# Splitting the value products of seven head groups by head and placing each head behind a quarter of a neighbouring projection

## The chip, the cores and the metric

One core of one Trainium2 chip. The metric is the time on the device of one execution, in microseconds (us). The kernel is written by hand: each engine has its own instruction stream, in an order fixed in the source, and the engines meet only through semaphores.

## What is computed

16 batches of x (256 tokens, 512 channels) go through three blocks, each followed by a residual sum and a layer norm (the inputs are float32):

```python
def _L0_attn_ref(h, Wq, bq, Wk, bk, Wv, bv, Wo, bo):        # 16 heads of 32 channels
    q, k, v = h @ Wq.T + bq, h @ Wk.T + bk, h @ Wv.T + bv   # (reshaped to heads)
    scores = jnp.einsum('bqhd,bkhd->bhqk', q, k) * scale    # causal
    attn = jax.nn.softmax(scores, axis=-1)
    o = jnp.einsum('bhqk,bkhd->bqhd', attn, v).reshape(B, S, H)
    return o @ Wo.T + bo

def _L0_ffn_ref(x, W_gate, W_qkv):                          # one shared key and value head
    indicator = one_hot(argmax(softmax(x @ W_gate.T)))
    q, k, v = jnp.split(x @ W_qkv.T, 3, axis=-1)
    k_shared = jnp.einsum('bth,bthd->btd', indicator, k)
    v_shared = jnp.einsum('bth,bthd->btd', indicator * top1_val, v)
    return causal_attention(q, k_shared, v_shared)

x = _layernorm(x + _L0_attn_ref(x, ...))
x = _layernorm(x + _L0_xattn_ref(...))     # a linear recurrence over time (wkv)
x = _layernorm(x + _L0_ffn_ref(x, ...))
```

## The kernel before

The program is a pipeline over batches. `iteration(t)` works on two of them at once: the first attention ("a", batch t) and the gated attention ("f", batch t-1), with the first projections of batch t+1 at its end. Iterations 1 to 14 have all three parts; the first and the last two lack some.

**What TensorE does.** In each iteration there are these kinds of work:

- Projections. One job is 12 matmuls of 512 columns (`tokens_out`) or 24 of 256 columns (`channels_out`), since each product is made of three: high by high, high by low and low by high part (`products`, L389 to L396). All of them write one PSUM bank, `pp`. The next job may start only when ScalarE and VectorE have taken the last one out of it: that is counted by `pa_free` (attention) and `pf_free` (gated). For a query or key job ScalarE writes the high part and then VectorE the low part (`qk_lo`, L1144). For the keys and values of the gated part VectorE multiplies by the gate (`pick`, L1202). For the output projection (`PA_WO`) VectorE adds the bank to the residual (`first_residual`, L1171). The second layer norm's result is transposed partly into `pp` too, and VectorE's second L1133 frees it. `PA_WO` waits besides for `a_free`: its moving side `k_lo` comes from L1157.
- Scores. There are four head groups of four heads in each attention. For each group the scores are made twice: in `sq` (L426 to L437) for the row maxima, which VectorE takes (L1015, then L1019 and L1020 for `neg_parts`); the maxima are transposed (`max_transpose`, L445), copied and carried into the operand by a DMA; and in `sk` (L461 to L472), of which ScalarE makes the exponentials (L819) into `prob0` and `prob1`.
- Values. One group is `values` (L476 to L490): for each of its four heads three float32 products of 33 columns (L484, L486, L488; each is two instructions in the trace), 24 instructions. They write `po`. VectorE then normalises (L1050, L1051), which counts `a_norm` or `f_norm`; in the gated part L1221 adds it to the residual (`third_residual`).
- Transposes of x, of y, of the outputs (L497) and of the shared key (L584, once for each iteration: its start serves below as the border of an iteration).

**What sets the order.** The order on each engine is that of the calls in `iteration`. SyncE's queue has the DMAs that stack q and k (L258) for the next batch, in a fixed order too. The value groups stand where they are called: a0 to a3 for the attention, f0 to f3 for the gated part. In an iteration from border to border the order of those with their neighbours is: a3 then `PF_V+1`; f0 then `PA_WO`; f1 then `PA_Q+1`; f2 then `PA_K+1`; f3, then the first scores of the next batch and `PA_V`; a0; a1 then `PF_Q`; a2 then `PF_K+1`.

Of the kernel before, what the change touches and what calls it, by code (L numbers as in the profile page):

```python
# [7 lines left out]
P = 128  # L8
CC = D // P
TT = S // P  # L10
NG = 4
# [28 lines left out]
def build(nc, x_d, xT_d, ctxT_d, weights_d, gate_d, ch_bias_d, row_bias_d, decay_d, first_d, out_d):  # L40
# [18 lines left out]
    with ctx:  # L59
# [328 lines left out]
        def _(pe):  # L388
            def products(out, lhs, rhs):  # L389

                for c in range(CC):
                    (lh, ll), (rh, rl) = lhs(c), rhs(c)
                    T.matmul(out, lh, rh, start=(c == 0), stop=False, skip_group_check=True)  # L393
                    T.matmul(out, lh, rl, start=False, stop=False, skip_group_check=True)  # L394
                    mm = T.matmul(out, ll, rh, start=False, stop=(c == CC - 1), skip_group_check=True)  # L395
                return mm  # L396
# [7 lines left out]
            def channels_out(w, pair):  # L404

                for i in range(2):
                    mm = products(pp[:, S * i:S * (i + 1)], weight(w, P * (2 * pair + i), P), tokens(0, S))
                return mm

            def tokens_out(bank, w, c, hi_t=xt_hi, lo_t=xt_lo):  # L410

                return products(bank[:, 0:D], tokens(P * c, P, hi_t, lo_t), weight(w, 0, D))
# [63 lines left out]
            def values(b, g, value, s_exp, s_norm, s_po):  # L476

                if g:
                    pe.wait_ge(s_norm, NG * b + g)
                pe.wait_ge(s_exp, TILES * b + 3 * (g + 1))  # L480
                out = po[:, 0:TT * HG * (HD + 1)].rearrange("p (c h d) -> p c h d", c=TT, h=HG)
                for k in range(HG):
                    h = HG * g + k
                    T.matmul(out[:, 0, k, :], prob0[:, k, 0:P], value(0, h),  # L484
                             start=True, stop=True, skip_group_check=True)
                    T.matmul(out[:, 1, k, :], prob0[:, k, P:S], value(0, h),  # L486
                             start=True, stop=False, skip_group_check=True)
                    mm = T.matmul(out[:, 1, k, :], prob1[:, k, :], value(1, h),  # L488
                                  start=False, stop=True, skip_group_check=True)
                mm.then_inc(s_po, 1)  # L490
# [51 lines left out]
            def project_a(b, job):  # L542

                weight_split(b, (W_Q, W_K, W_V, W_O)[job // 2])
                if job == PA_Q:
                    pe.wait_ge(xt_ready, b + 1)
                if job == PA_WO:

                    wait(pe, pf_free, PF_JOBS * b)

                    pe.wait_ge(a_free, A_JOBS * (b + 1))
                if job != PA_WO:
                    wait(pe, pa_free, PA_JOBS * b + job)
                if job < PA_K:
                    mm = channels_out(W_Q, job - PA_Q)
                elif job < PA_V:
                    mm = channels_out(W_K, job - PA_K)
                elif job < PA_WO:
                    mm = tokens_out(pp, W_V, job - PA_V)
                else:  # L560
                    mm = tokens_out(pp, W_O, job - PA_WO, k_hi, k_lo)
                mm.then_inc(pa_job, 1)

            def project_f(b, job):
# [6 lines left out]
                if job < PF_K:  # L571
                    mm = channels_out(W_FQ, job - PF_Q)
                elif job < PF_V:
                    mm = tokens_out(pp, W_FK, job - PF_K)
                else:
                    mm = tokens_out(pp, W_FV, job - PF_V)
                mm.then_inc(pf_job, 1)

# [41 lines left out]

            def values_a(b, g):
                values(b, g, value_a, a_exp, a_norm, a_po)

            def values_f(b, g):
                values(b, g, value_f, f_exp, f_norm, f_po)

            def iteration(t, do_a, prev, nxt):
# [65 lines left out]
                if do_a:  # L693
                    values_a(t, 3)
                if prev:
                    max_f(b, 0)
                    project_f(b, PF_V + 1)
# [10 lines left out]
                if prev:  # L708
# [6 lines left out]
                    values_f(b, 0)  # L715
                    if do_a:
                        max_f(b, 1, a_free, A_JOBS * a_done)
                if do_a:
                    project_a(t, PA_WO)
# [14 lines left out]
                if prev:  # L734
                    if not nxt:
                        max_f(b, 2)
                    values_f(b, 1)
                    if nxt:
                        max_f(b, 2)
                if nxt:  # L740
                    project_a(t + 1, PA_Q + 1)
# [11 lines left out]
                if prev:  # L753
                    if not nxt:
                        max_f(b, 3)
                    values_f(b, 2)
                    if nxt:
                        max_f(b, 3)
                if nxt:
                    project_a(t + 1, PA_K + 1)  # L760
                if prev:
# [3 lines left out]
                    values_f(b, 3)  # L765
# [6 lines left out]
                if nxt:  # L772
# [6 lines left out]
                    project_a(t + 1, PA_V)  # L779
# [789 lines left out]
```

## Time and profile before

| | |
|---|---|
| median of 3 runs | 1965.76 us (1945.75 to 1984.34) |
| profiled execution, span from first to last instruction | 1963.6 us; its own time is not listed apart; the span is 2.2 us under the median |
| TensorE | busy 1781.0 us, 91% |
| VectorE | busy 1268.9 us, 65% |
| ScalarE, GpSimdE | 24%, 27% |
| granted TensorE clock, mean | 0.837 |

PE is TensorE, PEld its weight loads, DVE VectorE, ACT ScalarE, POOL GpSimdE, SP SyncE. PEclk is the TensorE clock that was granted, as a share of full speed; it has two levels, 0.5 and 1.0 (1.2 and 2.4 GHz), so that a mean says how long each held. In a timeline row stand the start, the time taken, the engine, the line, the operation, what it writes and reads, and in brackets how long the engine stood idle before it and who released it.

### The profile page before, as it was taken

What the parts mean: (1) busy time and instruction counts of PE and PEld (TensorE: products, weight loads), DVE (VectorE), ACT (ScalarE), POOL (GpSimd) and SP (SyncE); (2) the same over time, 40 slices, a digit from 0 to 9 for tenths busy, and PEclk for the clock granted to TensorE, in tenths of its full rate; (3) what the DMA queues carried; (4) which work ended last, traced back from release to release, by engine and by line L of the source; (5) the groups of instructions that cost most, each with busy time, mean ns of one, the idle gap of its engine ahead of it and who ended that gap; (6) DMA issues with size and microseconds to landing.
All of it is one profiled execution on the core that took longest, in us unless ns stands there. A gap on an engine that the chain in (4) does not pass through costs nothing.

```text
span 1963.6 us, 33890 instructions
## 1 busy us (share of the span) xinstructions
PE 1781.0 (91%) x11904; PEld 1596.7 (81%) x11904; DVE 1268.9 (65%) x2678; ACT 477.5 (24%) x1040; POOL 521.0 (27%) x701
## 2 busy tenths in 40 slices
PE   5769989999999999999899999989899999999767
PEld 4658878888888888888888888878788888888656
DVE  3356766858576685757668575776848575685743
ACT  2232222313222132322222132221323132132201
POOL 1033230504133050323315041230505033050400
PEclk8679989788887878898797887988898886878675
DMA  5223122322213132221213222131322212131010
GB/s 139 82 62 82 42 77 50 81 59 62 73 25 79 42 81 59 62 62 33 75 49 81 59 62 54 41 82 42 81 59 62 73 38 60 49 81 50 6 43 12
DMA packets 61494, 118.30 MB, mean 60 GB/s; under 512 B 12688, under 2 KB 31120, under 8 KB 61456
## 3 DMA queue, kind: packets, MB, share of 16 engines
q1 hardware_dynamic: 61456, 117.79, 23.5%
q8 instruction: 24, 0.39, 0.1%
q14 instruction: 14, 0.11, 0.0%
HBM read 32.81 MB, written 8.39 MB: 21 GB/s over the span
## 4 chain that ended last, share of the span: by engine, by line
PE 71%; DVE 16%; issue 5%; DMA 3%; POOL 2%; ACT 2%; SPq 1%; DVEq 0%; POOLq 0%; ACTq 0%
PE pp L393 11%; PE pp L394 10%; PE pp L395 10%; PE po L488 6%; PE po L486 6%; PE po L484 6%; PE sq L434 4%; DVE neg_max L1015 4%; PE sq L426 3%; PE sk L461 3%; PE sk L469 2%; DVE neg_parts L1019 2%; PE sq L437 2%; DMA q_stack<-max_rows 1%; PE sq L429 1%
## 5 line engine op out<-in xcount | busy, mean ns | idle before, releaser
L819 ACT ACTIVATE prob<-sk 128x512 f32<-128x512 f32 x384 | 217.3, 597 | 799.9 <-PE sk L464 599.6
L1015 DVE TENSOR_REDUCE neg_max<-sq 128x2 f32<-128x512 f32 (+1 forms) x384 | 252.5, 679 | 82.3 <-PE sq L429 55.4
L393 PE MATMUL pp<-xt_hi,w_hi 128*128 128x256 f32 x768 | 235.0, 306 | 27.9 <-DVE w_lo L1002 14.4
L394 PE MATMUL pp<-xt_lo,w_hi 128*128 128x256 f32 x768 | 225.8, 294 | 0.0
L395 PE MATMUL pp<-xt_hi,w_lo 128*128 128x256 f32 x768 | 225.4, 294 | 0.0
L393 PE MATMUL pp<-w_hi,xt_hi 128*128 128x512 f32 x384 | 184.3, 480 | 7.7 <-DVE w_lo L1002 4.2
L393 PEld LDWEIGHTS pp<-xt_hi,w_hi 128*128 128x128 f32 x768 | 156.2, 203 | 33.1 <-issue 22.3
L394 PE MATMUL pp<-w_lo,xt_hi 128*128 128x512 f32 x384 | 173.2, 451 | 0.0
L395 PE MATMUL pp<-w_hi,xt_lo 128*128 128x512 f32 x384 | 170.6, 444 | 0.0
L1432 POOL TENSOR_TENSOR xt_lo<-x_raw,xt_hi 128x1024 fp32r<-128x1024 f32 x16 | 37.7, 2354 | 454.0 <-ACT xt_hi L857 454.0
L394 PEld LDWEIGHTS pp<-xt_lo,w_hi 128*128 128x128 f32 x768 | 156.3, 204 | 0.0
L395 PEld LDWEIGHTS pp<-xt_hi,w_lo 128*128 128x128 f32 x768 | 155.8, 203 | 0.0
L1111 DVE RECIPROCAL w_key<-w_key 128x256 f32<-128x256 f32 x64 | 111.2, 1737 | 18.2 <-POOL w_key L1459 18.2
L484 PE MATMUL po<-v_f,prob 128*128 128x33 f32 x512 | 109.0, 298 | 11.7 <-ACT prob L819 11.3
L1420 POOL TENSOR_TENSOR var_eps<-meanvar,eps 128x2 f32<-128x2 f32 x48 | 9.4, 197 | 411.7 <-DVE meanvar L1062 411.7
L488 PE MATMUL po<-v_a,prob 128*128 128x33 f32 x512 | 115.1, 311 | 0.0
L488 PE MATMUL po<-v_f,prob 128*128 128x33 f32 x512 | 114.2, 309 | 0.0
L484 PE MATMUL po<-v_a,prob 128*128 128x33 f32 x512 | 108.3, 297 | 6.1 <-ACT v_a L872 3.6
L486 PE MATMUL po<-v_a,prob 128*128 128x33 f32 x512 | 113.9, 308 | 0.0
L486 PE MATMUL po<-v_f,prob 128*128 128x33 f32 x512 | 112.7, 305 | 0.0
L393 PEld LDWEIGHTS pp<-w_hi,xt_hi 128*128 128x128 f32 x384 | 87.4, 228 | 28.2 <-DVE w_val L1202 4.6
L1427 POOL TENSOR_TENSOR xa<-xa,bo_row 128x512 f32<-128x512 f32 x32 | 40.3, 1282 | 259.1 <-DMA xa<-in_x 259.1
(162 smaller groups left out, 4247.2 us busy)
## 6 DMA issues: line engine op xcount, KB each, us to landing
q_stack<-q_hi SPq DMA_DIRECT2D x256, 128.0 KB, 2.3
q_stack<-q_lo SPq DMA_DIRECT2D x128, 128.0 KB, 2.3
k_stack<-k_hi SPq DMA_DIRECT2D x128, 128.0 KB, 2.3
x_raw<-in_xT SPq DMA_DIRECT2D x16, 512.0 KB, 3.5
k_stack<-k_lo SPq DMA_DIRECT2D x64, 128.0 KB, 2.3
xa<-in_x SPq DMA_DIRECT2D x16, 512.0 KB, 3.5
w_val<-in_ctxT SPq DMA_DIRECT2D x64, 128.0 KB, 2.1
out_y<-xb SPq DMA_DIRECT2D x16, 512.0 KB, 2.9
```

Of the source, the lines that this page charges most:

```text
L393: T.matmul(out, lh, rh, start=(c == 0), stop=False, skip_group_check=True)
L394: T.matmul(out, lh, rl, start=False, stop=False, skip_group_check=True)
L395: mm = T.matmul(out, ll, rh, start=False, stop=(c == CC - 1), skip_group_check=True)
L426: T.matmul(out[:, P * k:P * (k + 1)], q_stack[0:3 * HD, h, 0:P], key(h, 0, P, 3 * HD), start=(k == 0), stop=False, skip_group_check=True)
L434: T.matmul(out[:, S * k:S * (k + 1)], q_stack[0:3 * HD, h, P:S], key(h, 0, S, 3 * HD), start=(k == 0), stop=False, skip_group_check=True)
L461: T.matmul(out[:, S * k:S * (k + 1)], key(h, 0, P, rows), q_stack[0:rows, h, :], start=(k == 0), stop=False, skip_group_check=True)
L484: T.matmul(out[:, 0, k, :], prob0[:, k, 0:P], value(0, h), start=True, stop=True, skip_group_check=True)
L486: T.matmul(out[:, 1, k, :], prob0[:, k, P:S], value(0, h), start=True, stop=False, skip_group_check=True)
L488: mm = T.matmul(out[:, 1, k, :], prob1[:, k, :], value(1, h), start=False, stop=True, skip_group_check=True)
L819: A.activation(dst, sk[n % 2][:], ACT.Exp, scale=SCALE).then_inc(s_exp, 1)
L1015: V.tensor_reduce(dst, src, AX.X, ALU.max, negate=True).then_inc(s_max, 1)
L1111: V.reciprocal(w_key[:, c % HC, :], w_key[:, c % HC, :]).then_inc(w_rec, 1)
```

## The change

`values` is cut into `values_head(b, g, k)`: the three products of one head. `products` gets a `then`, which is called after each of the first three of its four contraction steps; `channels_out` calls it in the middle and at the end of its first half and in the middle of its second. `project_a` and `project_f` call the fourth head after the job's last matmul, and after its semaphore. So a head stands behind each quarter of the projection. The call that transposes the maxima (`max_f`) stands behind the first head (at a3) or the second (at f0, f1, f2). Group a0 stays as it was. f3 moves from ahead of the first scores of the next batch to `PA_V`, behind them.

```diff
-            def products(out, lhs, rhs):
+            def products(out, lhs, rhs, then=None):
...
                     mm = T.matmul(out, ll, rh, start=False, stop=(c == CC - 1), skip_group_check=True)
+                    if then is not None and c < CC - 1:
+                        then(c)
...
+            def channels_out(w, pair, then=None):
+
+                first = None if then is None else lambda c: then(0) if c == 1 else None
+                second = None if then is None else lambda c: then(2) if c == 1 else None
+                products(pp[:, 0:S], weight(w, P * (2 * pair), P), tokens(0, S), first)
+                if then is not None:
+                    then(1)
+                return products(pp[:, S:2 * S], weight(w, P * (2 * pair + 1), P), tokens(0, S), second)
...
+            def values_head(b, g, k, value, s_exp, s_norm, s_po):
+
+                if k == 0:
+                    if g:
+                        pe.wait_ge(s_norm, NG * b + g)
+                    pe.wait_ge(s_exp, TILES * b + 3 * (g + 1))
...
+                if k == HG - 1:
+                    mm.then_inc(s_po, 1)
...
                 mm.then_inc(pa_job, 1)
-
-            def project_f(b, job):
+                if then is not None:
+                    then(HG - 1)
...
                 if do_a:
-                    values_a(t, 1)
+                    if not prev:
+                        values_a(t, 1)
                     max_a(t, 2)
                 if prev:
-                    project_f(b, PF_Q)
+                    project_f(b, PF_Q, head_a(t, 1) if do_a else None)
...
-                    values_a(t, 2)
-                if prev:
-                    project_f(b, PF_K + 1)
+                    if not prev:
+                        values_a(t, 2)
+                if prev:
+                    project_f(b, PF_K + 1, head_a(t, 2) if do_a else None)
...
-                    project_a(t + 1, PA_V)
+                    project_a(t + 1, PA_V, head_f(b, 3) if prev else None)
```

TensorE's order in the loop body, at a2 and `PF_K+1`. Names: `pt` and `po` are PSUM banks, `v_a` the values. Before, the whole group stands between the transpose of the maxima and the projection that waits for `pf_free`:

```order
L445 MATMUL pt<-ident,neg_parts 16x128 [waits a_free,a_neg]
L484 MATMUL po<-v_a,prob 128x33 [waits a_exp,a_norm]
L486 MATMUL po<-v_a,prob 128x33
L488 MATMUL po<-v_a,prob 128x33
L484 MATMUL po<-v_a,prob 128x33
...
L488 MATMUL po<-v_a,prob 128x33
L393 MATMUL pp<-w_hi,xt_hi 128x512 [waits pf_free]
L394 MATMUL pp<-w_lo,xt_hi 128x512
```

After, the projection and its wait come right behind the transpose, and a head behind every three of its matmuls:

```order
L450 MATMUL pt<-ident,neg_parts 16x128 [waits a_free,a_neg]
L393 MATMUL pp<-w_hi,xt_hi 128x512 [waits pf_free]
L394 MATMUL pp<-w_lo,xt_hi 128x512
L395 MATMUL pp<-w_hi,xt_lo 128x512
L489 MATMUL po<-v_a,prob 128x33 [waits a_exp,a_norm]
L491 MATMUL po<-v_a,prob 128x33
L493 MATMUL po<-v_a,prob 128x33
L393 MATMUL pp<-w_hi,xt_hi 128x512
L394 MATMUL pp<-w_lo,xt_hi 128x512
```

The wait for `pf_free` has moved ahead of all twelve value products.

The same engine at f0 and `PA_WO`. Before, the group comes first and the projection waits behind it:

```order
L437 MATMUL sq<-mask_qk,ident_b 128x128 x2
L220 REGISTER_ALU
L712 REGISTER_ALU [waits a_norm]
L484 MATMUL po<-v_f,prob 128x33 [waits f_exp,dve_f]
L486 MATMUL po<-v_f,prob 128x33
...
L445 MATMUL pt<-ident,neg_parts 16x128 [waits a_free]
L220 REGISTER_ALU
L393 MATMUL pp<-w_hi,k_hi 128x512 [waits a_free,pf_free]
```

After:

```order
L746 REGISTER_ALU [waits a_norm]
L220 REGISTER_ALU [waits dve_f]
L557 REGISTER_ALU [waits pf_free]
L393 MATMUL pp<-w_hi,k_hi 128x512 [waits a_free]
L394 MATMUL pp<-w_lo,k_hi 128x512
L395 MATMUL pp<-w_hi,k_lo 128x512
L489 MATMUL po<-v_f,prob 128x33 [waits f_exp]
```

The waits for `pf_free` and for `a_free` (that is `k_lo`) now stand right behind the score products, ahead of every value product.

## Rows read from the trace of the kernel before

**Rows 1.** The page, busy time of each engine over the span.
```profile
PE 1781.0 (91%) x11904; PEld 1596.7 (81%) x11904; DVE 1268.9 (65%) x2678; ACT 477.5 (24%) x1040; POOL 521.0 (27%) x701
```

**Rows 2.** Two iterations and fourteen, windows: stretch, its length, busy us, PEclk.
```profile
1226.95:1336.86 109.91, 102.80 (x745) 91.15 (x744) 78.14 (x165) 28.56 (x63) 32.49 (x43) 0.92 0.25 63
1561.50:1681.00 119.50, 114.15 (x746) 103.13 (x745) 78.37 (x165) 28.77 (x63) 32.49 (x43) 0.81 0.23 58
198.40:1795.30 1596.90, 1516.03 (x10417) 1362.69 (x10416) 1089.33 (x2310) 401.25 (x882) 454.86 (x602) 0.86 0.24 61
```

**Rows 3.** Timeline at a3 and the projection behind it.
```profile
997.97 0.36 PE L484 MATMUL po<-v_a,prob 128*128 128x33 f32 x2
999.18 0.68 DVE L1202 TENSOR_TENSOR w_val<-pp,g_ind 128x512 f32<-128x512 f32 x1
1000.65 0.47 PE L393 MATMUL pp<-w_hi,xt_hi 128*128 128x512 f32 x1
1000.96 0.39 PE L394 MATMUL pp<-w_lo,xt_hi 128*128 128x512 f32 x1
```

**Rows 4.** Timeline at a2.
```profile
1098.11 0.31 PE L484 MATMUL po<-v_a,prob 128*128 128x33 f32 x2
1100.11 0.67 DVE L1202 TENSOR_TENSOR w_val<-pp,g_ind 128x512 f32<-128x512 f32 x1
```

**Rows 5.** Timeline at a1.
```profile
1309.60 0.31 PE L484 MATMUL po<-v_a,prob 128*128 128x33 f32 x2
1310.60 0.68 DVE L1133 TENSOR_TENSOR xt_lo<-pp,xt_hi 128x512 fp32r<-128x512 f32 x1
```

**Rows 6.** Timeline at f1 and at f2.
```profile
1022.33 0.31 PE L484 MATMUL po<-v_f,prob 128*128 128x33 f32 x2
1023.13 0.87 DVE L1144 SCALAR_TENSOR_TENSOR q_lo<-pp,ch_bias,q_hi 128x256 fp32r<-128x256 f32 x2
...
1034.67 0.31 PE L484 MATMUL po<-v_f,prob 128*128 128x33 f32 x2
1034.94 0.88 DVE L1144 SCALAR_TENSOR_TENSOR k_lo<-pp,ch_bias,k_hi 128x256 fp32r<-128x256 f32 x2 [0.33 <-ACT k_hi L866]
```

**Rows 7.** Timeline at f0.
```profile
1239.54 0.27 PE L484 MATMUL po<-v_f,prob 128*128 128x33 f32 x1
1240.43 2.36 DVE L1020 TENSOR_TENSOR neg_parts<-neg_max,neg_parts 128x8 fp32r<-128x8 f32 x1
1242.71 0.47 DVE L1157 SCALAR_TENSOR_TENSOR k_lo<-pt,ch_bias,k_hi 128x256 fp32r<-128x256 f32 x1
1243.24 0.28 PE L445 MATMUL pt<-ident,neg_parts 128*16 128x128 f32 x1 [0.86 <-DVE k_lo L1157]
```

**Rows 8.** Timeline at f3; the last row is the page's on DMA issues, us to landing last.
```profile
1043.71 0.41 PE L484 MATMUL po<-v_f,prob 128*128 128x33 f32 x2 [0.69 <-ACT prob L819]
1044.49 0.59 SPq L258 DMA_DIRECT2D k_stack<-k_hi  x1
1047.22 0.45 PE L426 MATMUL sq<-k_stack,q_stack 96*128 96x128 f32 x1
...
k_stack<-k_hi SPq DMA_DIRECT2D x128, 128.0 KB, 2.3
```

**Rows 9.** VectorE behind a gated value group: first and last of three.
```profile
1028.05 0.20 DVE L1050 RECIPROCAL o_rec<-po 128x8 f32<-128x8 f32 x1
1028.74 0.42 DVE L1221 TENSOR_TENSOR xb<-xb,o_tok 128x256 f32<-128x256 f32 x1
```

**Rows 10.** Windows: four neighbouring stretches of one iteration, cut where PEclk changed.
```profile
1045.53:1055.78 10.25, 9.83 (x40) 8.18 (x40) 9.17 (x19) 2.26 (x6) 5.01 (x7) 0.50 0.67 162
1055.80:1066.00 10.20, 8.20 (x58) 6.67 (x57) 8.47 (x17) 2.77 (x5) 8.56 (x14) 1.00 0.15 33
1066.01:1086.49 20.48, 20.48 (x105) 20.10 (x105) 9.07 (x22) 3.46 (x6) 0.90 (x2) 0.50 0.19 56
1086.50:1113.80 27.30, 26.90 (x205) 24.01 (x205) 15.68 (x38) 5.88 (x14) 2.51 (x2) 1.00 0.29 70
```

More of the change, by code:

```diff
@@ L402, in tokens, with tokens_out @@
                 return lambda c: (hi_t[:, c, lo:lo + n], lo_t[:, c, lo:lo + n])
[L404 to L412, printed above, removed]
+            def channels_out(w, pair, then=None):
[5 more added lines that the diff above has]
+                return products(pp[:, S:2 * S], weight(w, P * (2 * pair + 1), P), tokens(0, S), second)
+            def tokens_out(bank, w, c, hi_t=xt_hi, lo_t=xt_lo, then=None):
+                return products(bank[:, 0:D], tokens(P * c, P, hi_t, lo_t), weight(w, 0, D), then)
             def scores_sq(b, g, tiles, stk, per, key, s_sq, s_max):
@@ L554, in project_a, with project_f @@
                 if job < PA_K:
-                    mm = channels_out(W_Q, job - PA_Q)
+                    mm = channels_out(W_Q, job - PA_Q, then)
                 elif job < PA_V:
-                    mm = channels_out(W_K, job - PA_K)
+                    mm = channels_out(W_K, job - PA_K, then)
                 elif job < PA_WO:
-                    mm = tokens_out(pp, W_V, job - PA_V)
+                    mm = tokens_out(pp, W_V, job - PA_V, then=then)
                 else:
-                    mm = tokens_out(pp, W_O, job - PA_WO, k_hi, k_lo)
+                    mm = tokens_out(pp, W_O, job - PA_WO, k_hi, k_lo, then)
                 mm.then_inc(pa_job, 1)
-            def project_f(b, job):
+                if then is not None:
+                    then(HG - 1)
+            def project_f(b, job, then=None):
                 if job == PF_Q:
@@ L571, in project_f @@
                 if job < PF_K:
-                    mm = channels_out(W_FQ, job - PF_Q)
+                    mm = channels_out(W_FQ, job - PF_Q, then)
                 elif job < PF_V:
-                    mm = tokens_out(pp, W_FK, job - PF_K)
+                    mm = tokens_out(pp, W_FK, job - PF_K, then=then)
                 else:
-                    mm = tokens_out(pp, W_FV, job - PF_V)
+                    mm = tokens_out(pp, W_FV, job - PF_V, then=then)
                 mm.then_inc(pf_job, 1)
+                if then is not None:
+                    then(HG - 1)
             def key_transpose(b, s_before, before):
@@ L692, in iteration, with piece @@
                     sq_f(b, 0, 0, 1, 2)
-                if do_a:
+                if do_a and not prev:
                     values_a(t, 3)
                 if prev:
-                    max_f(b, 0)
-                    project_f(b, PF_V + 1)
+                    if do_a:
+                        turn_third = head_a(t, 3)
+                        def piece(k):
+                            turn_third(k)
+                            if k == 0:
+                                max_f(b, 0)
+                        project_f(b, PF_V + 1, piece)
+                    else:
+                        max_f(b, 0)
+                        project_f(b, PF_V + 1)
                     wait(pe, a_exp, TILES * a_done)
@@ L733, in iteration @@
                     x1_transpose(t, 0)
[L734 to L736 removed]
+                if prev and not nxt:
+                    max_f(b, 2)
                     values_f(b, 1)
[L738 to L739 removed]
                 if nxt:
[L741 removed]
+                    project_a(t + 1, PA_Q + 1, head_f(b, 1, lambda: max_f(b, 2)) if prev else None)
                 if prev:
```

54 lines of the change are left out of this document (27 added, 27 removed).

## The prediction

> **What bounds the kernel now.** I read the busy times of the engines first. TensorE is busy 91% of the span, VectorE 65% [rows 1]: the end is set by TensorE's own stream, and a wait put into it costs its full length unless it was idle there already. Then I read the windows of single iterations. One took 109.9 us with a granted clock of 0.92, another 119.5 us with 0.81; both have the same work [rows 2]. So there are two things to spend: time in which TensorE stands still, and time at its lower clock. With levels 1.0 and 0.5, a mean of 0.92 is 17.6 us at the lower level and 0.81 is 45.4 us. 9.6 us for 27.8 us makes 0.345 us lost for each us at the lower level, and 109.9 - 0.345 x 17.6 = 103.8 us for an iteration without any. The mean iteration is 1596.9 / 14 = 114.1 us, at 0.86, some 32 us of them at the lower level [rows 2]. All that a perfect clock could give back is therefore 10.3 us an iteration.
>
> Third, the timeline around the value groups. The reader is to see what lies under them. All projections share one PSUM bank. At a3 the group starts at 997.97, and VectorE's multiply that empties the bank ends at 999.86; the projection starts at 1000.65, without a wait [rows 3]. The group, 2.65 us long, is the cover under which the bank is emptied. It is so at every moved group but f3.
>
> **The change, part by part.** The number of instructions is the same. Each projection moves ahead of its value group, and its wait for the bank with it. Behind the waiting matmul everything on TensorE queues, the value products too, which could have run. The new wait is the time from the start of the group to the end of the emptying.
> - a3: 999.86 - 997.97 = 1.9 us [rows 3].
> - a2: the gate must be worked out before VectorE can multiply; 1100.78 - 1098.11 = 2.7 us [rows 4]. Here the group was just long enough.
> - a1: both halves of the transposed x must be split first; 1311.28 - 1309.60 = 1.7 us, less about 0.1 for a transpose of maxima that runs there: 1.6 us [rows 5].
> - f1 and f2: 1024.00 - 1022.33 = 1.7 us and 1035.82 - 1034.67 = 1.15 us, of which 0.15 was a wait before as well, so 1.0 us [rows 6].
> - f0: `PA_WO` needs `k_lo`, which ended 3.6 us after the group's start, because VectorE's L1020 took 2.36 us there. The group hid 2.7 of it, 0.86 was waited for [rows 7]. Now all of it is, and the group is still to run. Cost 2.3 us, taken a little under 2.7 for the iterations in which `k_lo` comes earlier.
> - f3: the first scores of the next batch need the stacked keys. The last of the three DMAs is issued at 1044.49 and takes 2.3 us to land: 1046.8. TensorE got there at 1047.22 [rows 8]. Without f3 it gets there by 1043.7 and waits. Only 0.4 us are won, and the group's 2.65 us (full clock) come back within `PA_V`: cost 2.2 us.
>
> The group's result comes later relative to its projection: the last head now stands behind the projection's end. VectorE's stream is in order, so what is queued behind the normalising comes later too. At f0 the residual that empties the bank after `PA_WO` stands behind three operations that take 1028.05 to 1029.16, 1.1 us [rows 9]; with 0.7 us of its own and the hand-overs, `PA_WO+1` is late by about 0.95. At a2 the next multiply stands behind two of them: `PF_V` late by 0.5. At a3 the same delays the maxima of f1: 0.75. At f3 the residual, the third norm's statistics and a division stand ahead of the next maxima: 1.5. Sum of the four 3.7 us, each bounded by zero where VectorE has slack and by these values where TensorE runs at full clock.
>
> At the lower clock TensorE gets later to each such place while VectorE and ScalarE take as long as before, so waits shrink. I count a3, a2, a1 and f3 whole (1.9 + 2.7 + 1.6 + 2.2 = 8.4) and f0, f1, f2 and the four late ones by half ((2.3 + 1.7 + 1.0 + 3.7) / 2 = 4.35): 12.7 us an iteration. The ends are 8.4 and 17.1. Nothing else is added: the transposes of the maxima move by at most one group, and all of these waits come ahead of them.
>
> Seams between values and projections rise from 7 to 28 an iteration. The first matmul behind a group holds its place for 0.31 us [rows 3], where the ones in a job run at 0.23 (2.8 us for 12), so leaving a group costs 0.08; a head entered from a projection can have its first weights ready and win as much. I take zero. The Trainium skill ("TensorE: Matmul & The Clock Gate", Step-by-step: what each phase is for) says that the next weights are loaded while the running matmul streams, which would favour mixing short products with long ones; by it 21 more entries at 0.08 would win 1.7 us an iteration, 25 us in all. The row shows the price at the exit, which cancels this.
>
> **The clock.** In the rows the clock fell in stretches where value products stood next to idle time: at 1045.5, within f3 after its 0.69 us wait, and at 1066.0, within a0, and it rose again inside a projection, at 1055.8 and 1086.5 [rows 8, 10]. The stretch 1055.8 to 1066.0 that ended with the fall had only 8.20 busy us in 10.20 [rows 10]. The change works both ways. It takes away pure value stretches, which is good at full clock. But each new wait of 1.6 us or more puts idle time next to them; and once the clock is low, the next projection is half value products, and so is no longer what has brought it back. It then has to wait for the next projection that is left whole. At the lower level 105 matmul records took 20.5 us, at the upper 205 took 27.3 [rows 10], 1.5 times as long on average, and at most twice. A mixed job of 5.5 us (2.8 and 2.65) then takes 8 to 11, I take 10, the score products up to the next whole projection 5 to 7, the part of that until it rises 4. If each place falls: a2 15 us (a whole projection is near); a3 30, since `PA_WO` is mixed as well; f1 17; f3 25; a0 32, through the transposes and `PF_Q`. That is 119 us. Not every place falls each time, so I take three quarters, 90 us. No row shows a mixed projection; the ends are zero and 119.
>
> **Sum.** 103.8 + 12.7 + 0.345 x 90 = 147.6 us an iteration against 114.1: 33.5 more. Fourteen iterations have all seven groups moved and the next one four, 14.6 in all: 489 us. 1963.6 + 489 = 2453 us of span; with the 2.2 us to the median 2455 us, 25% slower.
>
> **The rivals.**
> - *The waits come, the share of the lower clock stays as it is.* What the mixing saves then equals what the waits cost. Waits halfway between 12.7 and 17.1, 14.9 us: 1966 + 14.9 x 14.6 = 2183 us. For it: the value stretches themselves are where the clock fell in before.
> - *The waits come and the clock stays up.* 103.8 + 14.9 = 118.7 us, 4.6 more: 2033 us. The whole lower-clock time goes and doesn't pay for the waits. The skill's same page (HAM oscillation) says that long pauses between bursts throttle the engine, and by it waits as short as these would not; but here the clock fell without any long pause [rows 10], so I give it little.
> - *Faster.* The mixed stretches hold the full clock and the bank is emptied sooner than the rows say, because VectorE, with the same work in a less crowded order, is no longer behind when a projection ends: waits of 5 us in place of 12.7. 103.8 + 5 = 108.8 us: 1966 - 5.3 x 14.6 = 1889 us. It decides from the point where the waits are under 10.3 us and the clock never falls. Against it: at a3, a1, f1 and f2 the emptying is a chain of its own length behind a TensorE result, not a backlog.
> - *Cancelling.* Both near 10 us, within 2% of 1966.
> - *Worse still.* All 119 us at the lower clock and each costing 0.45: 103.8 + 12.7 + 53.6 = 170 us, 2783 us.
>
> **How the numbers follow.** Forecast (2300 to 2640) 0.66; share of the clock unchanged 0.17; clock up 0.07; faster 0.04; within 2% 0.03; above 2640 0.03. The range 2130 to 2640 leaves out the last four, 0.17. A measurement of this kernel tells about 2% from no change. Faster by over 2%: 0.04; within 2%: 0.03; slower by over 2%: 0.93.
>
> **What would show it.** Right: the first matmul of `PF_K+1`, `PF_V+1`, `PF_Q`, `PA_Q+1`, `PA_K+1` and `PA_WO` with idle time ahead of it, released by VectorE's L1202, L1133, L1144 and L1157, 1 to 3.6 us each; the first scores of the next batch waiting for a DMA into `k_stack`; the mean clock falling to about 0.7, and long stretches at 0.5 that begin at such a wait and end in a whole projection. Wrong: a clock of 0.86 or above with the waits there (then 2183 or 2033), or projections that start without a wait.

## The result, and the profile after

The changed kernel takes 2504.69 us (median of 4 runs, 2494.62 to 2509.33), the kernel before 1971.39 us beside it (4 runs, 1945.75 to 1984.34). The ratio is 1.290, with a 95% interval of 1.283 to 1.298: slower. (A ratio is taken without the executions that lie over 1.5% above the fastest of their kernel, so it need not equal the quotient of the two medians, 1.270 here.) The forecast was 2455 us, 25% slower.

The page of the kernel after: span, busy times, granted clock in 40 slices.

```profile
span 2492.8 us, 33877 instructions
...
PE 2126.3 (85%) x11904; PEld 1892.3 (76%) x11904; DVE 1271.6 (51%) x2678; ACT 488.5 (20%) x1040; POOL 511.7 (21%) x701
...
PEclk8587777676676667766667776766767667786665
```

Against [rows 1] TensorE has the same 11904 instructions, and yet 2126.3 us of busy time in place of 1781.0. That is not more work but the same work at a lower clock: the mean is 0.709 where it was 0.837. The rest is standing still: 2492.8 - 2126.3 = 366 us, where it was 1963.6 - 1781.0 = 183 us. VectorE has the same busy time as before, so nothing has become dearer there.

The same fourteen iterations as in the last row of [rows 2], in a window:

```profile
214.20:2316.94 2102.74, 1845.02 (x10418) 1644.50 (x10417) 1091.84 (x2310) 411.55 (x882) 445.28 (x602) 0.71 0.18 46
```

2102.74 / 14 = 150.2 us an iteration, against 114.06. Here 36.1 x 14 = 506 us of the 529 us that the span grew.

What TensorE waited for, over the whole span (us in total, times, longest), first after and then before:

```profile
PE pp L393 <- DVE w_val L1229: 68.5, 33, 2.6
PE sq L431 <- DMA k_stack<-k_hi: 65.3, 15, 5.5
PE pp L393 <- DVE k_lo L1184: 54.6, 16, 4.3
PE pp L393 <- DVE q_lo L1171: 28.3, 18, 2.0
PE pt L450 <- DVE neg_parts L1047: 19.3, 29, 2.1
PE pp L393 <- DVE xt_lo L1160: 17.8, 16, 1.5
...
PE pp L393 <- DVE k_lo L1171: 17.8, 16, 1.9
PE sq L439 <- DVE neg_max L1042: 13.1, 28, 1.2
```

```profile
PE sq L434 <- DVE neg_max L1015: 28.5, 51, 2.4
PE pt L445 <- DVE neg_parts L1020: 28.3, 35, 2.1
...
PE pt L445 <- DVE k_lo L1157: 9.1, 11, 1.0
...
PE sq L426 <- DMA k_stack<-k_hi: 7.2, 4, 5.5
```

The new rows are those with `pp` and L393, the first matmul of a projection, and the DMA into `k_stack`. They are the seven moved groups: `w_val` is a3 and a2, `k_lo` L1184 is f0 (before it was waited for by the transpose L445), `q_lo` f1, `xt_lo` a1, `k_lo` L1171 f2, `k_stack` f3. The rows on maxima fell, 28.5 + 28.3 to 13.1 + 19.3 us.

The waits of one iteration, in the timeline of TensorE (a3, f0, the second half of `PA_WO`, f1, f2, f3, a1, a2):

```profile
1274.77 0.80 PE L393 MATMUL pp<-w_hi,xt_hi 128*128 128x512 f32 x1 [1.79 <-DVE w_val L1229]
...
1294.93 0.80 PE L393 MATMUL pp<-w_hi,k_hi 128*128 128x512 f32 x1 [3.58 <-DVE k_lo L1184]
...
1305.70 0.50 PE L393 MATMUL pp<-w_hi,k_hi 128*128 128x512 f32 x1 [1.07 <-DVE xa L1198]
...
1315.76 0.39 PE L393 MATMUL pp<-xt_hi,w_hi 128*128 128x256 f32 x1 [1.56 <-DVE q_lo L1171]
...
1328.96 0.39 PE L393 MATMUL pp<-xt_hi,w_hi 128*128 128x256 f32 x1 [1.03 <-DVE k_lo L1171]
...
1341.05 1.11 PE L431 MATMUL sq<-k_stack,q_stack 96*128 96x128 f32 x4 [4.28 <-DMA k_stack<-k_hi]
...
1381.47 0.38 PE L393 MATMUL pp<-xt_hi,w_hi 128*128 128x256 f32 x1 [1.07 <-DVE xt_lo L1160]
...
1400.51 0.65 PE L393 MATMUL pp<-w_hi,xt_hi 128*128 128x512 f32 x1 [2.56 <-DVE w_val L1229]
```

Each is at the place that the forecast named. And the clock around the first of them, in windows:

```profile
1269.61:1274.30 4.69, 2.96 (x27) 2.36 (x25) 2.92 (x7) 0.60 (x1) 0.00 (x0) 1.00 0.37 84
1274.77:1302.00 27.23, 23.65 (x98) 20.99 (x98) 9.14 (x15) 3.10 (x5) 2.34 (x1) 0.51 0.10 29
1302.20:1339.00 36.80, 30.64 (x257) 28.55 (x256) 27.01 (x57) 11.52 (x27) 12.28 (x18) 1.00 0.11 24
```

The stretch ahead is at full clock. From the wait at a3 on it is at half, through the whole mixed `PF_V+1`, the score products, the wait at f0 and three quarters of the mixed `PA_WO`: 27 us, in which 98 records ran; the next 36.8 us took 257.

### The profile page after: what moved, and what is told of

Its sections match the earlier page's. It is cut to its first block, busy times and chain, and to the rows that moved or that the text cites. A ratio compares the mean times of both kernels' runs of the same rounds, so it can differ in the third digit from the quotient of the medians.

```text
span 2492.8 us, 33877 instructions
## 1 busy us (share of the span) xinstructions
PE 2126.3 (85%) x11904; PEld 1892.3 (76%) x11904; DVE 1271.6 (51%) x2678; ACT 488.5 (20%) x1040; POOL 511.7 (21%) x701
## 4 chain that ended last, share of the span: by engine, by line
PE 78%; DVE 14%; issue 3%; DMA 2%; ACT 2%; SPq 1%; POOL 1%; DVEq 0%; POOLq 0%; ACTq 0%
PE pp L393 14%; PE pp L394 11%; PE pp L395 11%; PE po L493 7%; PE po L491 7%; PE po L489 5%; PE sq L439 4%; PE sk L466 4%; PE sq L431 3%; DVE neg_max L1042 3%; PE sk L474 3%; PE sq L434 2%; PE sq L442 2%; DMA k_stack<-k_hi 2%; DVE neg_parts L1046 2%
## 5 line engine op out<-in xcount | busy, mean ns | idle before, releaser
L1077 DVE RECIPROCAL o_rec<-po 128x8 f32<-128x8 f32 x128 | 26.4, 206 | 583.3 <-PE po L493 583.3
L393 PE MATMUL pp<-xt_hi,w_hi 128*128 128x256 f32 x768 | 248.0, 323 | 79.7 <-DVE q_lo L1171 28.3
L393 PE MATMUL pp<-w_hi,xt_hi 128*128 128x512 f32 x384 | 238.2, 620 | 72.8 <-DVE w_val L1229 68.5
L393 PEld LDWEIGHTS pp<-xt_hi,w_hi 128*128 128x128 f32 x768 | 156.8, 204 | 93.2 <-DVE q_lo L1171 28.1
L394 PE MATMUL pp<-w_lo,xt_hi 128*128 128x512 f32 x384 | 206.4, 537 | 0.0
L395 PE MATMUL pp<-w_hi,xt_lo 128*128 128x512 f32 x384 | 205.9, 536 | 0.0
L393 PEld LDWEIGHTS pp<-w_hi,xt_hi 128*128 128x128 f32 x384 | 107.4, 280 | 92.7 <-DVE w_val L1229 71.8
L489 PEld LDWEIGHTS po<-v_a,prob 128*128 128x128 f32 x512 | 128.1, 274 | 40.9 <-issue 17.2
L489 PEld LDWEIGHTS po<-v_f,prob 128*128 128x128 f32 x512 | 123.6, 263 | 23.8 <-issue 2.0
L393 PE MATMUL pp<-w_hi,k_hi 128*128 128x512 f32 x128 | 84.7, 662 | 63.6 <-DVE k_lo L1184 54.6
L493 PE MATMUL po<-v_a,prob 128*128 128x33 f32 x512 | 136.2, 356 | 0.0
L491 PE MATMUL po<-v_a,prob 128*128 128x33 f32 x512 | 134.8, 353 | 0.0
L493 PE MATMUL po<-v_f,prob 128*128 128x33 f32 x512 | 129.9, 342 | 0.0
L491 PE MATMUL po<-v_f,prob 128*128 128x33 f32 x512 | 129.8, 342 | 0.0
```

What stands on the lines that cost most here:

```text
L489: T.matmul(out[:, 0, k, :], prob0[:, k, 0:P], value(0, h), start=True, stop=True, skip_group_check=True)
L491: T.matmul(out[:, 1, k, :], prob0[:, k, P:S], value(0, h), start=True, stop=False, skip_group_check=True)
```

## The experiments

Two numbers are taken from each trace besides the time. *Idle*: the waits in brackets of TensorE's rows, summed between the starts of the first and the fifteenth shared-key transpose and divided by fourteen. *Lower level*: 2 x (1 - mean clock) x length of an iteration, the mean from the clock record of the same stretch. A *fall* is one unbroken stretch at the lower level. Before has 5.5 us idle and 31.2 us at the lower level; after has 18.3 and 86.8. Both are read from the one profiled execution of each kernel; where its clock lies at one end of that kernel's executions, the others' clocks are given.

All variants come from the changed kernel, by a helper that puts the first `mode` heads of a group ahead of its projection and the others behind its quarters. 4 is the order before, 0 that of the change; "late" puts all four behind the undivided projection. Every variant computes all of the reference.

```diff
+            def placed(mode, head, project, turn=None, at=-1):
+                if mode == "late":
+                    if turn is not None:
+                        turn()
+                    project(lambda k: [head(h) for h in range(HG)] if k == HG - 1 else None)
+                    return
+                for k in range(mode):
+                    head(k)
+                if turn is not None and at < mode:
+                    turn()
...
+                project(piece if mode < HG else None)
```

**late: the waits without the mixing.**

```diff
+MODE = {'a1': 'late', 'a2': 'late', 'a3': 'late', 'f0': 'late', 'f1': 'late', 'f2': 'late', 'f3': 'late'}
```

> Every moved group stands whole behind its undivided projection: the new waits stay, the mixing goes. If the mixed projections are what keeps the clock low once it has fallen, a fall now ends inside the next projection: mean granted clock 0.79 or more, idle time of TensorE as in the changed kernel (350 to 380 us), time 2200 to 2320 us. If the waits alone set the clock and the mixing has no part in it, the clock stays near 0.71 and the time within 2% of 2504 us.

Measured 2341.16 us (2 runs), ratio 1.201 (1.178 to 1.224), clock 0.787. A few thousandths under the clock expected and 21 us above the top of the times. Its idle time is even more than after's, 21.4 us an iteration, since the transposes of the maxima lost their cover as well. At the lower level it has 56.1 us in place of 86.8. The number of falls tells how: 9.3 an iteration of 6 us each, where after has 4.7 of 18 us and before 3.7 of 8 us. One of them, around the same place as above (`PF_V+1` behind a3's scores), in late:

```profile
1190.90 0.28 PE L452 MATMUL pt<-ident,neg_parts 128*16 128x128 f32 x1 [1.19 <-DVE neg_parts L1084]
1191.50 0.58 PE L395 MATMUL pp<-w_hi,xt_hi 128*128 128x512 f32 x1 [0.32 <-DVE w_val L1266]
1191.89 0.63 PE L396 MATMUL pp<-w_lo,xt_hi 128*128 128x512 f32 x1
...
1194.87 0.54 PE L397 MATMUL pp<-w_hi,xt_lo 128*128 128x512 f32 x1
1195.26 0.39 PE L395 MATMUL pp<-w_hi,xt_hi 128*128 128x512 f32 x1
```

The step is 0.43 us from 1191.89 on and 0.23 from 1195.26 on: here the clock is low for 3.4 us and rises within the undivided projection. In after, at the mixed one, it stayed low for 27. So with more waits than before there are more falls, with mixing or without, and with the mixing each fall is long. The time at the lower level is smaller in late although it waits more, so the mixing has a part of its own in the clock.

**half: two heads ahead as cover, two mixed, f3 put back.**

```diff
+MODE = {'a1': 2, 'a2': 2, 'a3': 2, 'f0': 2, 'f1': 2, 'f2': 2, 'f3': 4}
```

> Six groups with two heads ahead of the projection and two behind its first two quarters; f3 back ahead of the scores. Two heads cover 1.33 us of each wait. If uncovered emptying of the bank is the cause, the waits fall to 0.5 at a3, 1.3 at a2, 0.3 at a1 and f1, none at f2 and some 2 at f0, 4 to 6 us an iteration with what comes late on VectorE; clock 0.76 to 0.84; 2020 to 2150 us. If mixing as such is what costs, half of the mixing in six of seven groups keeps about 3/7 of the 530 us: 2200 us or more.

Measured 2113.48 us (2 runs), ratio 1.084 (1.045 to 1.123), clock 0.797; idle 9.9 us, lower level 46.8 us. As expected: with 1.3 us of cover left, the waits shrink and do not vanish (the wait for `w_val` is 27.4 us in all in place of 68.5).

**One place alone.** a2, f2 and f3 each changed by itself, the other six as before.

```diff
+MODE = {'a1': 4, 'a2': 0, 'a3': 4, 'f0': 4, 'f1': 4, 'f2': 4, 'f3': 4}
```

> The change at a2 alone, where the wait is longest. Waits and clock: 2.6 us of wait an iteration and a fall at each, some 12 us more at the lower level (0.345 each): 6.7 us times 15 iterations, 2060 us (2030 to 2095). An equal share of the loss for each group (mixing as such): 76 us more, 2045 us; told apart by the next run.

> The change at f2 alone, where the wait is shortest (1.0 us, and no fall of the clock in the changed kernel). Waits and clock: 1.0 us an iteration less what the clock gains from one value stretch fewer: 1945 to 1990 us. An equal share of the loss for each group: 2045 us.

> The change at f3 alone. No drain of the bank is uncovered here, but the group no longer covers the DMAs of the stacked keys: 4 us of wait for k_stack appear ahead of the next batch's first scores and 3.4 us of values with their wait leave, the group comes back within PA_V; with PA_V half value products the fall of the clock that is there anyway lasts some 10 us longer. 2.2 + 0.42 x 10 = 6.4 us an iteration, 2060 us (2020 to 2100). If only the bank's emptying counts: no change, 1930 to 1990 us.

only_a2: 2061.9 us (2 runs), ratio 1.058 (1.037 to 1.078). Its wait at the place is 2.56 us; idle 8.0, lower level 39.0 us. only_f2: 1964.47 us (10 runs), ratio 1.010 (1.002 to 1.018). Its wait is there, 1.03 us, but the lower level is 26.3 us in place of 31.2, which pays for it. (The profiled execution has a clock of 0.857; over all ten executions the mean is 0.847, over the thirteen of before beside them 0.829. The medians of all executions, 1964.47 and 1979.38 us, stand the other way round than the ratio, so whether only_f2 is a per cent slower isn't settled.) only_f3: 2069.74 us (2 runs), ratio 1.054 (1.044 to 1.065), idle 8.3 and lower level 45.6 us. All three lie within the times expected. Their rows of the new waits, in that order:

```profile
916.57 0.59 PE L395 MATMUL pp<-w_hi,xt_hi 128*128 128x512 f32 x1 [2.56 <-DVE w_val L1266]
```

```profile
910.62 0.39 PE L395 MATMUL pp<-xt_hi,w_hi 128*128 128x256 f32 x1 [1.03 <-DVE k_lo L1208]
```

```profile
PE sq L433 <- DMA k_stack<-k_hi: 59.2, 15, 5.5
```

If the split itself cost the time, each place would have a seventh of the loss, some 75 us. That falls with f2, which has all of the split and only the smallest wait: its time is within about a per cent of before's. a2 and f3, which uncover 2.6 and 3.8 us, cost five to six per cent each.

**f0_back: f0 as before, the other six as changed.**

```diff
+MODE = {'a1': 0, 'a2': 0, 'a3': 0, 'f0': 4, 'f1': 0, 'f2': 0, 'f3': 0}
```

> The whole change, but f0 back ahead of PA_WO as before. Its wait for k_lo is hidden again but for 0.65 us: 2.8 us an iteration less idle. And the first whole projection behind the fall at a3 is now PA_WO itself, so that this stretch at the lower clock ends a mixed job earlier, 8 to 10 us: 0.42 each, 3.5 to 4 us. Together some 6.5 us an iteration, 95 to 100 us: 2410 us (2370 to 2440). If the clock depends on the waits alone: 2460 us.

Measured 2366.86 us (2 runs), ratio 1.210 (1.197 to 1.223), clock 0.746: 138 us less than after, and just under the range that was given. An iteration is 8.8 us shorter. The idle time fell by 2.4 us, the time at the lower level by 16.6 us. By the line worked out below that is 2.4 + 0.42 x 16.6 = 9.4 us, so a single place is worth more than I had put down for it, and most of that through the clock. The place is the expected one: from the border of an iteration to f1's projection, over a3 and `PA_WO`, the time at the lower level is 15.8 us an iteration in place of 29.7, 14 of the 16.6 us. The size was too small: 8 to 10 us were expected there.

**cover: keep enough heads ahead, mix only the rest.** If mixing itself is no loss at full clock, a version which uncovers no wait should be as fast as before, or faster.

```diff
+MODE = {'a1': 3, 'a2': 4, 'a3': 3, 'f0': 4, 'f1': 3, 'f2': 2, 'f3': 4}
```

> The mixing without new waits: at a1, a3 and f1 three heads ahead of the projection (2.0 us, the waits were 1.6 to 1.9) and one behind its first quarter, at f2 two and two (1.33 against 1.15); a2, f0 and f3 as before. If waits and the clock that follows them are the whole loss: TensorE idle under 110 us a run above or below that of before, clock 0.85 to 0.88, time 1925 to 1990 us. If mixing as such costs, five of 24 moved heads: 2040 us.

A miss: 2028.4 us (4 runs), ratio 1.031 (1.019 to 1.043), above the range. Its timeline at f2 tells why:

```profile
1072.94 0.31 PE L491 MATMUL po<-v_f,prob 128*128 128x33 f32 x2
...
1075.74 0.38 PE L452 MATMUL pt<-ident,neg_parts 128*16 128x128 f32 x1 [1.37 <-DVE neg_parts L1084]
1075.85 0.58 PE L395 MATMUL pp<-xt_hi,w_hi 128*128 128x256 f32 x1
1076.22 0.42 PE L396 MATMUL pp<-xt_lo,w_hi 128*128 128x256 f32 x1
```

And three windows around it:

```profile
1066.00:1075.70 9.70, 8.29 (x75) 7.75 (x74) 9.00 (x18) 5.76 (x15) 6.03 (x8) 1.00 0.36 81
1075.74:1099.71 23.97, 22.86 (x104) 20.81 (x104) 15.15 (x29) 5.48 (x13) 8.32 (x13) 0.50 0.32 77
1099.80:1113.00 13.20, 10.81 (x66) 8.85 (x64) 10.26 (x19) 2.77 (x5) 10.03 (x15) 0.87 0.14 31
```

I had sized the cover at f2 by the bank alone, 1.15 us. But the transpose of the maxima stands there too, and waits for VectorE's `neg_parts`. Two heads hide only 1.3 us of it; the other 1.37 us TensorE stood. The clock fell in that very place and stayed at 0.5 for 24 us, through the mixed projection, the scores and the whole of f3. In twelve of the fourteen iterations a fall began at this wait; eight of them took 24 us, four took 10. Idle time is 6.3 us an iteration, only 0.8 over before; lower level 45.3 us, 14 more. (The profiled execution has a clock of 0.798, the other three 0.801 to 0.813.)

**cover2: the same with f2 put back.**

```diff
+MODE = {'a1': 3, 'a2': 4, 'a3': 3, 'f0': 4, 'f1': 3, 'f2': 4, 'f3': 4}
```

> A cleaner test of mixing without a wait: at a1, a3 and f1 three heads ahead and one behind the first quarter; f2, a2, f0, f3 as before. In the earlier run f2 had two heads ahead, and the transpose of the maxima behind them waited 1.4 us for VectorE. Without that: TensorE idle 5 to 6 us an iteration as before, time 1935 to 1995 us, no difference that can be told. If a head inside a projection costs by itself, by keeping the clock low: 2000 us or more, with longer stretches at the lower clock behind a3.

Measured 1938.58 us (4 runs), ratio 0.983 (0.969 to 0.997); idle 5.7 us, lower level 20.7 us. Three mixed heads in an iteration with their waits covered are no loss, and a small gain. (The profiled execution has a clock of 0.868, the other three 0.825 to 0.858, so 20.7 us is at the low end.) One place, f2, parts this from cover: 90 us between the medians.

**spread, spread_again, spread2: heads earlier, not later.** Here no head goes behind the projection. One head of a group moves ahead instead, between the score products or ahead of the transposes; three remain as cover.

```diff
+EARLY = {'a1': 1, 'a3': 1, 'f1': 1, 'f2': 1}
...
+                if prev and nxt and EARLY["f1"]:
+                    head_f(b, 1)(0)
                 if do_a:
                     x1_transpose(t, 0)
```

> The other way to break up a value group: the first head of a1, a3, f1 and f2 stands one piece earlier, ahead of the transposes or the last score tile, the other three heads ahead of the projection as before, so that the bank is still covered by 2.0 us. Waits and clock: no new wait, pure value stretches of 2.0 instead of 2.65 us, at a3 a 0.35 us wait for VectorE is filled: 1915 to 1975 us, perhaps 1% faster than before. If the order of the small products doesn't matter where no wait is added: 1930 to 1990 us, no difference to be seen.

> The same kernel as in the run spread, to settle its gain: 1880 to 1940 us, 2 to 5% under the kernel before measured beside it. If that gain was the luck of a few executions: within 1% of it.

> a1 with one head ahead of the transposes, f1 and f2 with one ahead of the last score tile and one ahead of the transposes; a3 as before, since its transposed maxima came so late that 0.7 us of wait for their DMA appeared. No new wait; fewer falls of the clock than before: 1890 to 1960 us, as fast as or faster than the first spread. If the clock gained nothing from it: 1945 to 1990 us.

spread: 1881.85, 1904.57 and 1913.13 us, and one disturbed execution of 5081.51 us, so that no ratio was given; all three lie under the range that was expected. The same kernel again, spread_again: 1917.81 us (6 runs), ratio 0.981 (0.973 to 0.990), a gain just short of the 2 to 5% expected. Its waits have a new row, score products that wait for the DMA which carries the maxima:

```profile
PE sk L469 <- DMA q_stack<-max_rows: 14.1, 14, 2.4
```

Two of the 14 are in the start of the program; the other twelve stand 9 us into an iteration, right behind `PF_V+1` at a3, 0.70 to 0.85 us each. From the transpose of the maxima to the scores that need them only the projection is left to run, and it is 0.8 us too short for the DMA. spread2 takes the early head at a3 back, and moves two heads early at f1 and f2, one of them before the last tile of the scores: 1962.09 us (4 runs), ratio 1.006 (0.996 to 1.016), idle 6.8 us: just over its range. The gain is gone: at a3 the wait has gone, but one like it, of 0.67 to 0.77 us, has come some 40 us into each iteration, and the row on `neg_max` is 31.7 us where spread_again has 19.8.

**joined: what each of the two kinds did best.** At a1, f1 and f2 one head early and three as cover. At a3 three as cover and one behind the first quarter of the projection, and so behind the transpose of the maxima, where its 0.6 us lengthen the way to the scores that spread found 0.8 us short.

```diff
+MODE = {'a1': 4, 'a2': 4, 'a3': 3, 'f0': 4, 'f1': 4, 'f2': 4, 'f3': 4}
+EARLY = {'a1': 1, 'a3': 0, 'f1': 1, 'f2': 1}
```

> The two arrangements that lost no time put together: one head ahead of the transposes at a1, f1 and f2, and at a3 three heads ahead of the projection and one behind its first quarter. TensorE idle near 5 us an iteration, the clock 0.87 to 0.90: 1885 to 1940 us. If the gains don't add: as spread, 1918 us, or between it and the kernel before.

Measured 1887.53 us (6 runs, 1878.51 to 1896.45) against 1963.28 us, ratio 0.965 (0.958 to 0.971). This beats both kernels. Its page:

```profile
PE 1720.7 (91%) x11904; PEld 1543.0 (81%) x11904; DVE 1247.3 (66%) x2678; ACT 476.9 (25%) x1040; POOL 521.0 (27%) x701
...
PEclk8679989899798989879898987989898897889575
```

The wait for the maxima's DMA is gone from all iterations but one (0.27 us there). Idle time is 4.8 us an iteration and the lower level 22.2 us, against 5.5 and 31.2: most of the 4.6 us by which its iteration is shorter (109.5 us) comes from the clock. Why the clock is better is not shown. The 0.65 us of idle time an iteration at f0 that before spends on `k_lo` are gone too, and none of VectorE's operations on the maxima is held up by GpSimdE there, as is told under f0 below.

**All of them in one line.** If waiting and clock are all there is, the iteration is a constant, plus the idle time, plus a price for each us at the lower level. With 0.42 for the price:

| kernel | iteration | idle | lower level | iteration - idle - 0.42 x lower |
|---|---|---|---|---|
| before | 114.1 | 5.5 | 31.2 | 95.5 |
| after | 150.2 | 18.3 | 86.8 | 95.4 |
| late | 139.9 | 21.4 | 56.1 | 94.9 |
| f0_back | 141.4 | 15.9 | 70.2 | 96.0 |
| half | 125.6 | 9.9 | 46.8 | 96.0 |
| only_f3 | 122.2 | 8.3 | 45.6 | 94.7 |
| only_a2 | 120.5 | 8.0 | 39.0 | 96.1 |
| cover | 120.3 | 6.3 | 45.3 | 95.0 |
| only_f2 | 113.0 | 6.7 | 26.3 | 95.3 |
| cover2 | 109.8 | 5.7 | 20.7 | 95.4 |
| joined | 109.5 | 4.8 | 22.2 | 95.4 |
| spread | 110.2 | 5.2 | 23.7 | 95.0 |
| spread_again | 111.8 | 5.1 | 27.6 | 95.1 |
| spread2 | 113.3 | 6.8 | 27.1 | 95.1 |

The last column stays within 94.7 to 96.1 over kernels with 0 to 28 mixed heads an iteration. There is no third cost that grows with the mixing. 0.42 was chosen so that before and after agree; the other twelve had no part in it. The thirteen executions of before that ran beside late give the price a second time, with no variant in it: the shortest (1929.94 us, mean clock 0.854) has 563 us at the lower level, the longest (2020.44 us, 0.807) has 779, and 0.42 x 216 = 91 us is what parts them. The line is an account and no cause: an iteration less its idle time is TensorE's busy time, and the line says that this changes with the clock alone. What moves the clock is for late, f0_back and cover to say.

## Why the prediction was right, step by step

By that line the 36.1 us that an iteration grew are 12.8 us of idle time and 0.42 x 55.6 = 23.3 us of clock.

- **The mechanism** (an in-order wait goes ahead of its cover): right at all seven places; only_a2 and only_f2 show it one by one.
- **The sum of the waits**: 12.7 us forecast, 12.8 measured. That these two meet is luck. Over the fourteen iterations the seven places came to 14.3 us more, where I had counted 10.9; everything else came to 1.5 us less, where I had counted 1.85 more. a3 and a2 together are 4.3 us an iteration (forecast 1.9 + 2.7). f1, f2 and a1 are 1.6, 1.0 and 1.1 us: f1 and f2, which I counted by half (0.85 and 0.5), came in full; a1 (1.6) came short.
- **f0**, 2.3 us counted by half: mis-sized. 3.47 us an iteration, less 0.65 before, is +2.8. I had halved it because at the lower clock TensorE gets there later. But its cover has gone altogether, and what it waits for is VectorE's stream, which takes as long at any clock (1271.6 us busy at a clock of 0.709, 1268.9 at 0.837). More than half of this wait is one small operation of VectorE that ran beside a large one of GpSimdE:

```profile
1291.92 2.34 POOL L1459 TENSOR_TENSOR xt_lo<-x_raw,xt_hi 128x1024 fp32r<-128x1024 f32 x1 [50.26 <-ACT xt_hi L884]
1292.12 2.16 DVE L1046 CAST neg_parts<-neg_max 128x8 fp32r<-128x8 f32 x1
```

  The usual length of that cast is 0.17 us. The 2.36 us of L1020 in [rows 7] stand beside the same subtraction on GpSimdE. An operation on `neg_parts` took 1.7 us or more fourteen times in after and eleven times in before, each time beside it, and never over 0.65 us otherwise.
- **f3**, 2.2 us: mis-sized too. 4.28 us an iteration, less 0.12 before, is +4.2 us (both without the 5.5 us at the program's start); the wait of 0.7 for `prob` that stood ahead of the group in [rows 8] went with it, which leaves +3.5. only_f3, with nothing else changed, has +2.8 us of idle time (8.3 - 5.5). The 2.2 us were the end's delay in an iteration in which the clock fell within f3, so that the group took 3.5 us there (1043.71 to 1047.22) in place of 2.65: I had set a place at the lower level against one at full clock, and counted the lower level a second time in the clock's term.
- **The late results**, 3.7 us by half: mostly wrong. Only `PA_WO+1` came, 1.07 us in the iteration shown (0.55 in the mean, 0.95 forecast), and with it one that I had not named: a0's values wait for ScalarE's `v_a`, 0.75 us an iteration in place of 0.22. `PF_V` does not wait. The maxima of f1 and of the next batch, for which I had 0.75 and 1.5, do not wait longer but less: the rows on `neg_max` and `neg_parts` fell by 24.4 us in all, 1.6 an iteration. Each new wait is a pause in which VectorE catches up, and the later waits behind it shrink: only_f3, with one new wait, has 18.5 + 17.2 us in these rows where before has 28.3 + 28.5. These errors, with those of f0 and f3, cancel in the sum.
- **The seams**, zero: right. At full clock in after a quarter of a mixed projection and a head:

```profile
1302.22 0.48 PE L393 MATMUL pp<-w_hi,k_hi 128*128 128x512 f32 x1
1302.54 0.40 PE L394 MATMUL pp<-w_lo,k_hi 128*128 128x512 f32 x1
1302.77 0.40 PE L395 MATMUL pp<-w_hi,k_lo 128*128 128x512 f32 x1
1302.77 0.42 PEld L489 LDWEIGHTS po<-v_f,prob 128*128 128x128 f32 x2
1303.00 0.30 PE L489 MATMUL po<-v_f,prob 128*128 128x33 f32 x2
...
1303.59 0.48 PE L466 MATMUL sk<-q_stack,kf_stack 98*128 98x256 f32 x2
```

  The quarter takes 1303.00 - 1302.22 = 0.78 us (unmixed 2.8 / 4 = 0.70), the head 1303.59 - 1303.00 = 0.59 (2.65 / 4 = 0.66). What the entry wins the exit gives back, as I had it. The rule of the Trainium skill ("TensorE: Matmul & The Clock Gate", Step-by-step: what each phase is for), that the next weights load while the running matmul streams, agrees with this trace: the head's first weight load starts at 1302.77, with the last matmul of the quarter. It brings nothing in the sum. The constant column above says the same over 28 heads.
- **The time at the lower level**, 90 us: right, 86.8, though the mix of places was another. In the iteration shown, falls began at a3, at the `k_stack` wait, at 1370.0 and at a2, and took 27.3, 27.3, 10.2 and 13.7 us, where I had 30, 25, 32 and 15; at f1, f2 and a1 the clock stayed up. The step behind it, "the next projection is half value products, and so is no longer what has brought it back", is what late against after shows. It is no law: in this iteration the clock rose inside the mixed `PA_WO` at 1302.
- **Its price**, 0.345 us for one us: mis-sized, 0.42. I had it from two iterations of before, with one difference of 9.6 us for 27.8. But the two differ in idle time as well, and [rows 2] show it: 109.91 - 102.80 = 7.1 us in one, 119.50 - 114.15 = 5.35 in the other. The busy times alone give 11.35 / 27.8 = 0.41. 0.42 x 86.8 = 36.5 us stands where I had 0.345 x 90 = 31.0: 5.4 us an iteration, 79 us in all, the largest single error. The base of 103.8 us was worked out with the same price; by the table it is 95.4 + 5.5 = 100.9, and so gave 2.9 us an iteration back. Together these two are the 2.6 us by which 147.6 stood short of 150.2.

The rival "waits come, share of the clock stays" (2183 us) falls with the clock of 0.709. The rule that I weighed against my own step (the Trainium skill, "TensorE: Matmul & The Clock Gate", HAM oscillation: long pauses between bursts throttle the engine) is not enough here, since the clock fell beside short waits too. In cover one wait of 1.37 us stood where the clock fell, in late one of 1.19 us and one of 0.32 us. Two waits of an iteration are long, 3.6 us at f0 and 4.3 for `k_stack`, and there the clock fell too or was down already. If the waits had left the clock alone, the time would have been near 2033 us.

The page "Perfetto Trace Analysis" of the Trainium skill says (Matmuls) that independent groups should rotate through different PSUM banks, so that one is emptied beneath the next group's products. All projections here share one bank, and the value group did that office; the 1.0 to 2.6 us at the first matmul of each but the first `PA_WO` are what emptying it costs in the open. (The 3.6 us at `PA_WO` are for `k_lo` and the 4.3 us at f3 for a DMA, so they are no matter of the bank.) A second bank for the projections wasn't tried.

What stays open: why falls begin at one wait and not at another of the same length, and what sets how long they last. Over the fourteen iterations of after the place decides, not the length of the wait. While the wait ran or within 2 us behind it, the clock fell each time at a3 (1.79 us), at a2 (2.56) and at the `k_stack` wait (4.3), and in none of the 28 waits at f1 (1.56) and f2 (1.03). It fell behind a0's wait of 0.77 us in all thirteen of after that were over 0.7 us, and behind none of the six such waits in cover2. The traces show where falls begin and end, and not why.

## What to carry to other kernels

Where an engine works in order, a small group between two jobs that share one buffer is not filler: it is the cover under which the buffer is emptied. Before moving it, subtract the start of the group from the end of the emptying; that wait comes in full, and at each place all waits that the cover hides must be counted, not only the buffer's (cover had left out the maxima). Spare products are better moved ahead, between other work that doesn't wait, and no more of them than the cover can spare.

A wait can cost more than its length where the clock falls beside it: here 12.8 us of it came with 23.3 us of clock. Read idle time and time at the lower level apart, for each variant, before deciding what a seam costs.

## What the hardware showed that I had not expected

- Small waits can count in the clock out of proportion. cover has 0.5 us more idle time an iteration than cover2 and 24.6 us more at the lower level; but the two traces lie at opposite ends of their kernels' clocks, and by the mean clocks of all four executions of each (0.806 and 0.850) it is some 14 us. The 90 us between the medians fit the latter: (0.5 + 0.42 x 14) x 14.6 = 93.
- An operation of VectorE that takes 0.17 us took 1.7 to 2.4 us where it ran beside a 2.3 us operation of GpSimdE, and TensorE's longest wait for VectorE in an iteration hangs on it.
- Falls of the clock are long where short and long products alternate: in after, of 46 between 300 and 1700 us, fifteen took 27 us or more; in late, of 92, none took over 14; in before, of 48, none over 21.
- The same kernel scatters by up to 2.5% either way from run to run (before: 1929.94 to 2020.44 us in one series of 13). That scatter is the clock's: in all thirteen, the span less 0.42 x the time at the lower level is 1689 to 1694 us.
